# A fused attention and feed-forward block on one core: ScalarE centres the rows, and VectorE's queue is put in another order

## The reference, cut to what matters

```python
x = x + conv_ref(ln_c(x))            # x: (16, 512, 24, 8); ln_c: layer norm over the 512 channels
t = to_tokens(x)                     # (16, 192, 512)
t = t + ffn_ref(ln_t(t), w1, w2)     # ln_t: layer norm over the 512 channels of a token
# conv_ref: channel gate from the mean and maximum over the tokens (fc1, relu, fc2, sigmoid),
#           token gate from mean and maximum over the channels (7x7 convolution, sigmoid)
# ffn_ref:  h = gelu(bitlinear(x, w1)); out = bitlinear(h, w2)
def bitlinear(x, w):                 # w: rounded to -1, 0, 1 times a unit
    scale = 127.0 / maximum(max(abs(x), axis=-1), 1e-5)
    xq = clip(round(x * scale), -128, 127) / scale
    return einsum('bsd,fd->bsf', xq, w_quant)
```

## Time and profile before

| | us |
|---|---|
| median of 3 runs (lowest, highest) | 311.19 (310.03, 312.21) |
| the profiled execution | 311.29 |
| its span, first to last instruction | 309.3 |
| PE, DVE, ACT, POOL busy | 265.9, 249.7, 217.1, 165.6 |

### The profile page before, as it was taken

How to read it: one execution, slowest core, us unless ns; L and a number is a source line. 1 busy time by engine, 2 the same in 40 slices (tenths; PEclk the granted TensorE clock), 3 DMA queues, 4 the chain that set the end, 5 groups by cost and what they waited for, 6 DMA issues and landing times.

```text
span 309.3 us, 5830 instructions
## 1 busy us (share of the span) xinstructions
PE 265.9 (86%) x1826; PEld 153.4 (50%) x1834; DVE 249.7 (81%) x556; ACT 217.1 (70%) x442; POOL 165.6 (54%) x267
## 2 busy tenths in 40 slices
PE   2457659696699999999999999999999987999974
PEld 2345634564356465645565555555555544444431
DVE  0673889989699989998998999899989997788410
ACT  1863687579476978687778876787678846676831
POOL 9506655416855385648555765566656563346410
PEclk9999965969999999999999999999999999899998
DMA  7999100002253129412931393439223713073693
GB/s 202 389 392 401 45 1 0 2 2 57 42 141 70 24 46 246 96 34 54 252 72 35 69 237 70 37 69 256 53 50 72 151 39 68 17 174 72 74 209 102
DMA packets 71077, 34.19 MB, mean 111 GB/s; under 512 B 52040, under 2 KB 68424, under 8 KB 70536
## 3 DMA queue, kind: packets, MB, share of 16 engines
q1 hardware_dynamic: 69300, 32.78, 43.1%
q10 hardware_dynamic: 1748, 1.05, 1.2%
HBM read 14.94 MB, written 6.29 MB: 69 GB/s over the span
## 4 chain that ended last, share of the span: by engine, by line
DVE 40%; PE 36%; issue 10%; ACT 4%; POOL 4%; ACTq 2%; DMA 1%; another core or an unknown queue 1%; SPq 1%; DVEq 0%; POOLq 0%
PE ps_o L1201 12%; DVE amax L883 8%; PE ps_h L1190 6%; PE ps_t L1190 6%; DVE t L856 6%; PE front L1120 3%; DVE st L858 3%; DVE amax L869 3%; DVE pv L824 3%; PE small L1166 2%; DVE cen L868 2%; DVE junk_v L909 2%; DVE st L782 2%; PE front L1210 2%; DVE res L900 2%
## 5 line engine op out<-in xcount | busy, mean ns | idle before, releaser
L1201 PE MATMUL ps_o<-w2T,hq 128*128 128x512 f16 x384 | 92.7, 379 | 1.1 <-DMA hq<-w_raw 1.1
L488 POOL TENSOR_SCALAR w_room<-w_room,q 128x1024 f32<-128x1024 f32 x48 | 57.1, 1201 | 51.4 <-DVE q L893 50.9
L883 DVE TENSOR_REDUCE amax<-w_room 128x1 f32<-128x1024 f32 (+1 forms) x48 | 57.2, 1208 | 2.3 <-ACT w_room L550 2.2
L1190 PE MATMUL ps_h<-w1T,xq 128*128 128x512 f16 x208 | 54.0, 403 | 1.1 <-ACT xq L550 0.7
L1201 PEld LDWEIGHTS ps_o<-w2T,hq 128*128 128x128 f16 x384 | 36.3, 98 | 36.0 <-DMA hq<-w_raw 2.1
L550 ACT ACTIVATE w_raw<-w_room 128x1024 f16<-128x1024 f16 x48 | 50.4, 1052 | 0.6 <-POOL w_room L488 0.6
L550 ACT ACTIVATE w_room<-ps_h,s 128x512 f32<-128x512 f32 x52 | 35.0, 688 | 13.1 <-PE ps_h L1190 12.0
L1190 PE MATMUL ps_t<-w1T,xq 128*128 128x512 f16 x176 | 42.0, 382 | 0.0
L550 ACT ACTIVATE w_room<-ps_t,s 128x512 f32<-128x512 f32 x44 | 30.2, 687 | 8.0 <-PE ps_t L1190 5.6
L1190 PEld LDWEIGHTS ps_h<-w1T,xq 128*128 128x128 f16 x208 | 20.1, 103 | 23.9 <-issue 3.9
L550 ACT ACTIVATE junk_m<-front 128x192 bf16<-128x192 f32 x64 | 20.6, 332 | 14.7 <-DVE pooled L795 14.7
(11 more groups left out here) (125 smaller groups left out, 450.5 us busy)
## 6 DMA issues: line engine op xcount, KB each, us to landing
out<-w_room SPq DMA_DIRECT2D x16, 384.0 KB, 3.0
x_in<-in_x SPq DMA_DIRECT2D x14, 384.0 KB, 5.1
w_room<-in_L_ffn_w SPq DMA_DIRECT2D x4, 1024.0 KB, 8.8
w_raw<-in_L_ffn_w SPq DMA_DIRECT2D x4, 1024.0 KB, 12.0
x_in<-in_x ACTq DMA_DIRECT2D x2, 384.0 KB, 3.8
hq<-w_raw SPq DMA_TRANSPOSE x48, 3.1
fc_raw<-in_L_conv_fc_w ACTq DMA_DIRECT2D x2, 128.0 KB, 4.2
taps_rev<-in_L_conv_sa_w SPq DMA_DIRECT2D x1, 0.2 KB
```

Source lines behind the costliest of these rows:

```text
L488: pool.tensor_scalar(part, part, q2[tile.par][:, 0:1], MAGIC, ALU.mult, ALU.add).then_inc(g_rounded, 1)
L883: chain.mark(dve.tensor_reduce(amax2[:, i:i + 1], w1_room[:, first + i * F // 2:first + (i + 1) * F // 2 + i], AX.X, ALU.max, apply_absolu ...
L1190: last = pe.matmul(banks[b], xq[tile.pair.par][:, tile.s, k, :], w1T[:, k, b * 512:(b + 1) * 512], start=(k == 0), stop=(k == NC - 1))
L1201: last = pe.matmul(ps_o[:, :], hq[tile.par][:, k, :], w2T[:, k, :], start=(k == 0), stop=(k == NF - 1))
```

## The change

ACT gets a new `centre(tile)` (activation Identity, scale -1, bias the mean, so it writes mean - t), announced by `cen_ready`, at three places of each body. DVE's `centre` becomes `limit`: it waits for `cen_ready`, then does what stood behind the subtraction, with -127 in place of 127. `add_attention` is split: the addition, and `row_stats`. DVE's list is put in another order; POOL's, ACT's and PE's have a few swaps.

```diff
 (ACT)
+            def centre(tile):
+                wait(act, stats2_ready, tile.at(1, 1))
+                wait(act, xq_turned, tile.at(1, -1))
+                copy(cen[tile.par][:, :], t[tile.pair.par][:, tile.s, :], cen_ready, ACT.Identity, scale=-1.0,
+                     bias=mv2[tile.par][:, 0:1])
 (ACT, prologue)
-            copy_weights(0, (4, 5, 6, 7))
+            copy_weights(0, (4, 5, 6))
+            centre(Tile(pair0, 0))
+            copy_weights(0, (7,))
...
-            gelu(Tile(pair0, 1), None, h_start, (2, 3))
+            gelu(Tile(pair0, 1), None, h_start, (2,))
+            centre(Tile(pair0, 2))
+            gelu(Tile(pair0, 1), None, h_start, (3,))
 (ACT, body)
-                gelu(Tile(pair, 2), nxt if normalise else None)
+                gelu(Tile(pair, 2), nxt if normalise else None, blocks=(0, 1, 2))
+                if normalise:
+                    centre(Tile(nxt, 0))
+                gelu(Tile(pair, 2), blocks=(3,))
...
-                    gelu(Tile(nxt, 0))
+                    gelu(Tile(nxt, 0), blocks=(0,))
+                    centre(Tile(nxt, 1))
+                    gelu(Tile(nxt, 0), blocks=(1, 2, 3))
...
                     copy_xq(Tile(nxt, 1), XQ_BANK[1])
+                if normalise:
+                    centre(Tile(nxt, 2))
                 if attend:
                     gate_channels(att)
...
                     pack_g(Tile(nxt, 0), 0)
+                if attend:
+                    sum_channels(Tile(att, 2))
                 copy_out(Tile(pair, 1), OUT_BANK[2])
-                if attend:
-                    sum_channels(Tile(att, 2))
 (DVE)
-                wait(dve, xq_turned, tile.at(1, -1))
-                link(dve.tensor_scalar(c[:, :], t_tile, mv2[tile.par][:, 0:1], None, ALU.subtract))
+                wait(dve, cen_ready, tile.at(1, 1))
                 link(dve.tensor_reduce(amax1[:, :], c[:, :], AX.X, ALU.max, apply_absolute_value=True))
 (POOL, body)
                     round_x(Tile(nxt, 0))
+                    rstd2(Tile(nxt, 1))
                 round_g(Tile(pair, 2))
                 if normalise:
-                    rstd2(Tile(nxt, 1))
                     round_x(Tile(nxt, 1))
+                    rstd2(Tile(nxt, 2))
                     round_g(Tile(nxt, 0))
-                    rstd2(Tile(nxt, 2))
 (PE, body)
-                    ffn_in(Tile(nxt, 1), blocks=(0, 1))
+                    ffn_in(Tile(nxt, 1), blocks=(0,))
                 if attend:
                     turn_ca(att)
                 if normalise:
-                    ffn_in(Tile(nxt, 1), blocks=(2, 3))
+                    ffn_in(Tile(nxt, 1), blocks=(1, 2))
...                 (spread_ca of tiles 0 and 1 of att)
+                    ffn_in(Tile(nxt, 1), blocks=(3,))
                 ffn_out(Tile(pair, 2), (0,))
...
+                ffn_out(Tile(pair, 2), (3,))
                 if normalise:
                     a = turn_xq(Tile(nxt, 2), XQ_BANK[2], a)
-                ffn_out(Tile(pair, 2), (3,))
```

More of the change, by code:

```diff
@@ L675, in _ @@
             token_mean(pair1, 3, 1)
+            centre(Tile(pair0, 1))
             copy_weights(1, (2, 3))
@@ L727, in body @@
                 if normalise:
-                    gelu(Tile(nxt, 1), blocks=(0, 1))
+                    gelu(Tile(nxt, 1), blocks=(0,))
                 if attend:
@@ L731, in body @@
                 if normalise:
-                    gelu(Tile(nxt, 1), blocks=(2, 3))
+                    gelu(Tile(nxt, 1), blocks=(1, 2, 3))
                 if attend:
@@ L855, in add_attention, with row_stats, limit @@
                 wait(dve, res_ready, tile.at(1, 1 - 2 * NT))
[L856 to L858 removed]
+                chain.mark(dve.scalar_tensor_tensor(t_tile, pv[par][:, s, :], sg[par][:, s:s + 1],
+                                                    xt[par][:, s, :], ALU.mult, ALU.add))
+            def row_stats(tile):
+                chain.wait()
+                link(dve.bn_stats(st2[:, :], t[tile.pair.par][:, tile.s, :]))
                 wait(dve, rs2_ready, tile.at(1, -1))
                 dve.bn_aggr(mv2[tile.par][:, :], st2[:, :]).then_inc(stats2_ready, 1)
[L862 to L866, removed]
[L867 to L868 removed]
+            def limit(tile):
+                c = cen[tile.par]
+                wait(dve, cen_ready, tile.at(1, 1))
                 link(dve.tensor_reduce(amax1[:, :], c[:, :], AX.X, ALU.max, apply_absolute_value=True))
@@ L1000, in _ @@
             add_attention(Tile(pair0, 0))
-            centre(Tile(pair0, 0))
+            row_stats(Tile(pair0, 0))
+            limit(Tile(pair0, 0))
             token_max(pair1, 0, 1)
@@ L1016, in _ @@
             hidden(pair1)
-            centre(Tile(pair0, 1))
+            limit(Tile(pair0, 1))
             split_gate(pair1)
@@ L1026, in _ @@
             add_attention(Tile(pair0, 2))
-            centre(Tile(pair0, 2))
+            row_stats(Tile(pair0, 2))
+            limit(Tile(pair0, 2))
             hidden_max(Tile(pair0, 1), 0)
@@ L1043, in body @@
                     add_attention(Tile(nxt, 0))
-                    centre(Tile(nxt, 0))
+                    row_stats(Tile(nxt, 0))
+                hidden_max(Tile(pair, 2), 0)
+                if normalise:
+                    limit(Tile(nxt, 0))
                 if attend:
                     token_max(att, 0, V1_BANK[0])
-                hidden_max(Tile(pair, 2), 0)
                 if attend:
@@ L1050, in body @@
                 hidden_max(Tile(pair, 2), 1)
-                hidden_scale(Tile(pair, 2))
+                if normalise:
+                    add_attention(Tile(nxt, 1))
                 if attend:
                     token_max(att, 2, V1_BANK[2])
+                if normalise:
+                    row_stats(Tile(nxt, 1))
+                hidden_scale(Tile(pair, 2))
                 add_ffn(Tile(pair, 0))
                 if normalise:
-                    add_attention(Tile(nxt, 1))
-                    centre(Tile(nxt, 1))
+                    hidden_max(Tile(nxt, 0), 0)
+                    limit(Tile(nxt, 1))
                 if attend:
@@ L1061, in body @@
                 if normalise:
-                    hidden_max(Tile(nxt, 0), 0)
+                    add_attention(Tile(nxt, 2))
+                if attend:
+                    hidden(att)
+                if normalise:
+                    row_stats(Tile(nxt, 2))
                     hidden_max(Tile(nxt, 0), 1)
                 if attend:
-                    hidden(att)
+                    split_gate(att)
                 if normalise:
@@ L1070, in body @@
                 if normalise:
-                    add_attention(Tile(nxt, 2))
-                if attend:
[L1073 to L1076, removed]
+                    limit(Tile(nxt, 2))
                 if attend:
@@ L1079, in body @@
                     scale_channels(Tile(att, 1), CA_BANK[1])
-                if turn:
-                    channel_stats(fresh, 0, 1)
+                if normalise:
+                    hidden_max(Tile(nxt, 1), 0)
                 if attend:
@@ L1084, in body @@
                 if turn:
+                    channel_stats(fresh, 0, 1)
                     aggregate(fresh, 0, 1)
+                if attend:
+                    split_stats(att)
                 if normalise:
@@ L1094, in body @@
                     sum_conv(att)
+                add_ffn(Tile(pair, 2))
                 if turn:
```

12 lines of the change are left out of this document (5 added, 7 removed).

## The result

The changed kernel takes 307.63 us, the one before 311.28 on the same chips: the ratio is 0.989 (95% interval 0.986 to 0.993), 3.65 us faster. Forecast were 7.6 us, so the direction was right and the size was twice too large. The profiled execution took 307.39 us, with a span of 305.5 against 309.3.

What follows compares the result with a forecast made beforehand. PE and DVE were nearly full, with PE waiting for DVE. Prologue -0.5, c = 1 to 4 -4.0, body 5 -2.4, clock -1.7 and c = 6 +1.0 gave -7.6, so 303.7 us; 8-in-10 range 300.5 to 310.

Steps and rivals of the forecast that it cites:

- What bounds the kernel, and what goes: Full bodies: PE stands three times for DVE, 1.27 us; these waits go, and tile 1's addition loses 0.8 us.
- Body 5: Body c = 5: of 2.84 us of shown PE idle time 0.4 stays, so -2.4 us.
- turn_xq behind the last quarter: End of c = 6, with no convolution to cover turn_xq: a new PE gap of 0.85 us.
- Table loads: ACT: Identity is in every table set, so no loads beyond the two already shown.
- D: Rival, ACT: Identity is not in Gelu's and Tanh's table, two loads for each of 24 centres, 372 us; chance 0.01.
- Prologue and body 0: Start of the kernel: the prologue costs +0.4 us, body 0 gains -0.9, together -0.5.
- I take 0.3 us a body for all new waits: Full bodies: they take 29.3 us, 1.0 saved in each, 4.0 for c = 1 to 4.
- The chain to v: Head of a body: POOL's v ends within -0.1 and +0.4 us of PE's turn, its wait replacing the copy_out wait.
- the clock, -1.7: Body 6: without the 1.41 us wait ahead of it, no low clock is expected, -1.7 us.
- in c = 6 ... 1.0: Body 6: 0.85 us at its end and a small wait for xq earlier cost 1.0 us together.
- Rival A: Centres at the head of ACT's queue delay Gelu blocks and copies, 0.5 us a body more: 306.7 us; chance 0.25.
- C: Rival, body's head: POOL's v 1.6 us late in six bodies, 313.3 us, or 315 with low clock; chance 0.08.

Runs made afterwards that it cites:

- e7: The changed kernel with turn_xq(nxt,2) back ahead of ffn_out's last quarter in body 6 alone: 306.86 us, ratio 0.986.
- the two profiles of before: The kernel before the change, profiled twice; it was run again unchanged for the second profile, at 310.19 us.
- e10: The changed kernel with the edits of e6 and e7 and load_x first in SyncE's list of a body: 303.62 us, ratio 0.974.
- e4: On top of e3, POOL does normalise1(fresh,2), which gives v, ahead of the half round_g(nxt,1): 306.46 us, ratio 0.985.
- e5: On top of e4, ScalarE does copy_out(pair-1,2) ahead of pack_g(pair,1,0): 307.27 us, ratio 0.987.
- the first three edits: e3, e4 and e5, each on top of the last, on the changed kernel: 307.36, 306.46 and 307.27 us.
- the fourth: e6, on top of the three edits before it: 309.29 us, ratio 0.993.
- e9: The kernel before the change, with POOL computing v of tile 2 twice: 310.13 us, ratio 0.996.
- e3: The changed kernel with DVE's aggregate(fresh,2) back ahead of add_ffn: 307.36 us, ratio 0.989.
- e6: On top of e5, ScalarE's pack_g(pair,1,1) moved behind copy_xq(nxt,0): 309.29 us, ratio 0.993.

## Why the prediction was right and wrong, by its steps

**Right.** *What bounds the kernel, and what goes.* All three waits of PE for DVE went from a full body, the addition of tile 1 fell from 1.56 to 0.74, and DVE has room (26.04 of 29.77 us busy). *Body 5*: 29.22 in place of 31.32, -2.1 for -2.4. *turn_xq behind the last quarter*: 0.85 us at the seam, shown by e7. *Table loads*: two, as before; D is out.

**Partly right.** *Prologue and body 0.* Body 0 gained the 0.9 of the forecast (31.10 us against 32.04 and 32.01). The prologue cost more than 0.4: body 0 starts at 78.41 us, and at 77.40 and 77.91 in the two profiles of before. So body 1 starts at 109.51 against 109.44 and 109.92: +0.1 or -0.4 for a forecast of -0.5.

**Wrong, the largest step: "I take 0.3 us a body for all new waits".** They are 0.9 us, so c = 1 to 4 saved 0.51 each, 2.0 in place of 4.0. What went was a little more than the 1.27 us of the forecast. It overlooked a fourth wait, ahead of spread_ca(att,2): 0.61 us after turn_res starts (194.55) before the change, 0.44 after it.

```profile
195.16 0.38 PE L1152 MATMUL front<-caT,img_pick 128*128 128x512 bf16 x1
```
```profile
193.85 0.60 PE L1238 MATMUL front<-id,res 128*128 128x128 f32 x4
194.29 0.38 PE L1180 MATMUL front<-caT,img_pick 128*128 128x512 bf16 x1
```

So 1.44 us went and 0.9 came. The floor is then 28.8 us and not 29.0; e10 has the same, 29.12 less 0.32. Two things in the step failed. The chain to v was given between -0.1 and +0.4 us and taken in the middle; it came at +0.47, just beyond its upper end, because two bn_stats and an aggregate now stand behind scale(att,2) ahead of everything that POOL does up to v. The forecast had these terms in its chain; which of them it took too short can't be told, as it gives only their end. And v's wait was to replace ScalarE's: it came on top for half of it, since DVE's gate, stretched to 0.71 us beside round_g, and Identity, at 0.72, push ScalarE's packing, copy_out and token_mean back as well. The lateness has two causes side by side: POOL's v (e4: 0.13 us of a body by itself), and ScalarE's chain (e10 against e5: 0.5 once the packing is later and the loads no longer wait for it).

**Right in kind, too sure in size: "the clock, -1.7".** Against the first profile of before the term came out, 24.39 us with the low clock against 22.70 without. Against the second there was nothing to win. The low clock in body 6 went with the wait of 1.41 us, but in two of four profiles only, so the change takes away the chance of a loss and not a sure 1.7 us; which part of it the median of before holds is not known.

**Wrong: "in c = 6 ... 1.0".** At full clock the body went from 22.70 to 24.53, +1.8: 0.85 at the seam, the rest in two waits of turn_xq for cen, 0.46 and 0.17 us in brackets and 0.62 and 0.34 by the starts. In a body without attention work the new order puts a maximum of 1.18 us between statistics and limit with nothing gained, and tile 0's addition lands on the later round_g and takes 1.57 us, 0.75 before. The forecast took 0.15 for all this.

Against the first profile: +0.1 (start of body 1), -2.0 (c = 1 to 4), -2.1 (c = 5), +0.1 (c = 6: -1.7 for the clock, +1.8), +0.1 behind it: -3.8, as the spans say. Of the 3.8 us that are missing, 2.0 are the new waits of c = 1 to 4, 0.8 body 6, 0.6 the prologue and body 0, and 0.4 the rest. Rival A's time, 306.7, is the nearest, and its mechanism is half of it; C's mechanism, POOL's v, is the other half at a third of its dose.

## What to carry to other kernels

When a wait is taken from an engine that feeds the bound, list the chains that end within some tenths of a microsecond of the same place, on every engine, and the queues that they pass: here v, ScalarE's copies and SyncE's loads stood one behind the other, and the first three edits added 0 to 0.13 us a body each, the fourth took back more than it gave, and with the loads moved all together gave 0.65. Moving an operation to another engine and reordering around its latency is one change; neither half says what the whole is worth. A term for a lowered clock that one profile shows may be a matter of that execution: take a second profile before it goes into the sum in full.

## What the runs showed of the hardware that was not expected

A doubled POOL instruction did not make the kernel before slower: a full body took 30.16 us in place of 30.28, and the whole 310.13, a ratio of 0.996 (0.994 to 0.999), of which the fall of the clock may be a part (e9, at full clock in body 6, has a span of 307.6 us; the profile of before that was at full clock there too has 308.2). A VectorE addition of 0.75 us took 1.56 or 0.74 depending on which of the two engines got there first. The Trainium skill has the rule for it (SBUF — State Buffer, Who interferes with whom: who issues first holds the ports for the whole instruction). The traces agree, also for a small tensor_scalar: token_gate on three columns took 0.71 us beside round_g after the change, 0.65 in e3, where round_g had less left to run, and 0.16 in e4, where round_g stands elsewhere. TensorE's clock fell to 1.2 GHz after a wait of 1.41 us in two executions and did not in two others, with the same wait; in e6 it fell after one of 1.72 us, at a cost of 1.66 us.
